# A six-layer windowed-attention stage in a new order of nine turns, with the queries' rotary halves added by an accumulating transfer

## What is computed

```python
def attn_layer(x, Wqkv, qs, ksc, Wo):            # 16 heads of 64, x first goes through shift_tokens
    q, k, v = jnp.split(x @ Wqkv, 3, -1)         # 128 -> 3 * 1024
    q = l2norm(q) * qs
    k = l2norm(k) * ksc
    q = q * cos * scale + rotate_half(q) * sin * scale
    k = k * cos * inv + rotate_half(k) * sin * inv
    out = local_attention(q, k, v)               # softmax over causal keys in a window of 32
    return out @ Wo

def ffn_layer(x, g, bln, W1, b1, W2, b2):        # x again through shift_tokens
    xn = (x - mu) / jnp.sqrt(var + 1e-05) * g + bln
    a, gate = jnp.split(xn @ W1 + b1, 2, -1)
    return a * jax.nn.gelu(gate, approximate=False) @ W2 + b2
```

## Time and profile before

| what | us |
|---|---|
| median of 2 runs | 3666.64 |
| lowest and highest | 3664.30, 3668.97 |
| the profiled execution, its own time | 3660.63 |
| span of the profiled execution | 3658.8 |
| granted TensorE clock, mean over the span | 0.991 of full speed |

### The profile page before, as it was taken

How to read it: one execution, slowest core, us unless ns; L and a number is a source line. 1 busy time by engine, 2 the same in 40 slices (tenths; PEclk the granted TensorE clock), 3 DMA queues, 4 the chain that set the end, 5 groups by cost and what they waited for, 6 DMA issues and landing times.

```text
span 3658.8 us, 125829 instructions
## 1 busy us (share of the span) xinstructions
PE 3573.9 (98%) x51141; PEld 2639.5 (72%) x51141; DVE 2813.3 (77%) x5297; ACT 2925.6 (80%) x5539; POOL 2587.4 (71%) x4812
## 2 busy tenths in 40 slices
PE   8989997999999999999999999999999999999997
PEld 6777884777777777777777777777777777777776
DVE  6834446888888888888888888888888888888884
ACT  5756664888888888888888888888888888888886
POOL 5522225777777777777777777777777777777773
PEclk9999999999999999999999999999999999999998
DMA  3000000000000000000000010000000000000000
GB/s 98 3 11 8 8 5 18 18 10 11 11 16 25 18 11 11 10 25 25 11 10 10 17 26 18 10 10 11 25 25 10 10 11 16 14 13 13 17 13 14
DMA packets 145113, 59.13 MB, mean 16 GB/s; under 512 B 117017, under 2 KB 139294, under 8 KB 144542
## 3 DMA queue, kind: packets, MB, share of 16 engines
q1 hardware_dynamic: 143820, 50.88, 5.6%
q10 hardware_dynamic: 722, 0.21, 0.0%
HBM read 23.95 MB, written 2.10 MB: 7 GB/s over the span
## 4 chain that ended last, share of the span: by engine, by line
PE 82%; DVE 1%; POOL 1%; ACT 0%; issue 0%; DMA 0%; SPq 0%; POOLq 0%; DVEq 0%
PE bank L1048 18%; PE bank L1021 11%; PE bank L1195 10%; PE bank L1100 10%; PE bank L1163 7%; PE bank L1179 6%; PE bank L1131 5%; PE bank L1116 5%; PE bank L1133 4%; PE bank L1039 3%; PE bank L1111 2%; DVE R L1353 0%; DVE ss L1368 0%; DMA ys<-Y 0%; POOL R L1466 0%
## 5 line engine op out<-in xcount | busy, mean ns | idle before, releaser
L1353 DVE TENSOR_TENSOR R<-bank,tables 128x1024 f32<-128x1024 f32 x768 | 903.5, 1218 | 218.6 <-ACT sq L1255 218.4
L1048 PE MATMUL bank<-WA,xcT 128*128 128x512 f32 x1536 | 693.9, 594 | 4.3 <-ACT xcT L1229 2.4
L1255 ACT ACTIVATE sq<-bank 128x512 f32<-128x512 f32 x768 | 459.2, 598 | 159.1 <-PE bank L1048 159.1
L1048 PEld LDWEIGHTS bank<-WA,xcT 128*128 128x128 f32 x1536 | 277.2, 190 | 283.2 <-issue 279.4
L1458 POOL TENSOR_TENSOR R<-R 128x512 f32<-128x512 f32 x384 | 480.4, 1272 | 0.0
L1368 DVE TENSOR_REDUCE ss<-sq 128x16 f32<-128x1024 f32 x384 | 459.8, 1198 | 0.2 <-issue 0.2
L1100 PE MATMUL bank<-WV,xcT 128*64 128x512 f32 x1536 | 414.2, 618 | 0.0
L1478 POOL TENSOR_TENSOR P<-P,inv_sum 128x512 f32<-128x512 f32 x384 | 401.6, 1046 | 0.7 <-DVE inv_sum L1408 0.7
L1472 POOL TENSOR_TENSOR P<-P,rn 128x512 f32<-128x512 f32 x384 | 402.0, 1047 | 0.0
L1195 PE MATMUL bank<-WO,OT 128*128 128x128 f32 x3072 | 396.8, 283 | 0.0
L1466 POOL TENSOR_TENSOR R<-R,rn 128x512 f32<-128x512 f32 x384 | 391.8, 1041 | 0.0
(11 more groups left out here) (157 smaller groups left out, 7819.6 us busy)
## 6 DMA issues: line engine op xcount, KB each, us to landing
WA<-in_wqkv SPq DMA_DIRECT2D x24, 256.0 KB, 2.9
ystat<-Y SPq DMA_DIRECT2D x192, 32.0 KB
ystat<-Y SPq DMA_DIRECT2D x384, 15.8 KB
ys<-Y SPq DMA_DIRECT2D x192, 32.0 KB
ys<-Y SPq DMA_DIRECT2D x384, 15.8 KB
WV<-in_wqkv SPq DMA_DIRECT2D x6, 512.0 KB, 3.8
WO<-in_wo SPq DMA_DIRECT2D x6, 512.0 KB, 4.5
X<-in_x SPq DMA_DIRECT2D x4, 512.0 KB, 5.2
```

Source lines behind the costliest of these rows:

```text
L1048: mm(b[QK_BANK[n, half]][:, :], m.xsT[:, k % 2, :], cols[:, half, :, :], start=True, stop=True)\
L1255: nc.scalar.activation(by_half[:, half, :, :], b[QK_BANK[n, half]][:, :].rearrange("p (h d) -> p h d", d=32), ACT.Square)\
L1353: tt(both, src.unsqueeze(1).to_broadcast([128, 2, 16, 32]), tab.unsqueeze(2).to_broadcast([128, 2, 16, 32]), ALU.mult).then_inc(s.rotated, 1)
```

## The change

The third stage is written anew; the first two stages are the same.

- **Queries' parts.** PE's accumulating second transposes are gone. Instead POOL issues one transfer in each turn, `queries_added`, which adds `R[:, QUERIES, 1, :]` onto `R[:, QUERIES, 0, :]` (128 partitions of 1024 fp32, 512 KB) with `accum_op`; `queries_turned`(i-1) waits for it one turn later and has eight passes instead of sixteen. `R` for the queries has one buffer, so the next tile's `rotary` waits for `queries_turned` half 0.
- **Keys' parts** are still added by two POOL instructions, but POOL scales the keys in the same turn i rather than at the head of turn i+1.
- **Order.** Every engine's list is new, PSUM's banks are assigned anew, and the pipeline is one turn deeper (LAST = 8, and the lists run for N + 9 turns).
- **Waits.** Semaphores with two or four parts in a turn are counted by a small class, and the increments `hold` are gone.

```diff
-FIRST, LAST = 0, 7
...
+LAST = 8
...
-    QK_BANK = {(QUERIES, 0): 1, (KEYS, 1): 0, (QUERIES, 1): 4, (KEYS, 0): 3}
-    TURNED_IN, TURNED_OUT = b[3], b[6]
-    KT_BANK, QT_BANK, V_BANK = (b[2], b[1]), (b[4], b[7]), (b[6], b[5])
-    S_BANK, PT_BANK, PV_BANK = (b[2], b[1]), (b[5], b[7]), (b[5], b[2])
-    OUT, FF_BANK, FF_OUT = b[1], (b[0], b[3], b[4]), b[0]
+    QK_BANK = {(QUERIES, 0): 3, (QUERIES, 1): 6, (KEYS, 0): 1, (KEYS, 1): 2}
+    TURNED_IN, TURNED_OUT = b[4], b[6]
+    KT_BANK, QT_BANK, V_BANK = (b[7], b[0]), (b[7], b[4]), (b[1], b[4])
+    S_BANK, PT_BANK, PV_BANK = (b[5], b[6]), (b[0], b[0]), (b[4], b[3])
+    OUT, FF_BANK, FF_OUT = b[0], (b[2], b[1], b[7]), b[5]
...
+            def queries_turned(t, j):
+                if exists(t):
+                    pe.wait_ge(s.q_added, 16 * t + 16)
+                    if j == 0:
+                        at_least(pe, s.h, 3 * (t - 6))
+                    elif t == N - 1:
+                        pe.wait_ge(s.v_copied.sem, s.v_copied.upto(1, t + 1))
                     for n in range(4):
...
+                        at = j * 512 + n * 128
+                        last = turned(QT_BANK[j][:, n * 128:(n + 1) * 128], m.R[:, QUERIES, 0, at:at + 128])
+                    last.then_inc(s.q_turned.sem, 1)
...
-                    for n in range(4):
-                        at, col = j * 512 + n * 128, n * 128
-                        mm(QT_BANK[j][:, col:col + 128], m.R[:, QUERIES, 0, at:at + 128], m.ident[:, :], is_transpose=True,
-                           start=True, stop=False)
-                        last = mm(QT_BANK[j][:, col:col + 128], m.R[:, QUERIES, 1, at:at + 128], m.ident[:, :],
-                                  is_transpose=True, start=False, stop=True)
-                    last.then_inc(s.q_turned, 1)
...
+            for i in range(N + LAST + 1):
+                input_turned(i)
+                out_projection(i - 5)
+                queries(i, 0)
+                queries_turned(i - 1, 1)
+                queries(i, 1)
+                queries_turned(i - 1, 0)
+                keys(i, 0)
+                keys(i, 1)
+                keys_turned(i - 1, 1)
+                keys_turned(i - 1, 0)
+                ff_out(i - 8)
+                probs_turned(i - 3, 1)
+                normal_turned(i - 6)
+                head_outputs(i - 4)
+                scores(i - 1)
+                values(i, 0)
+                values(i, 1)
+                probs_turned(i - 3, 0)
+                ff_in(i - 7)
...
+            for i in range(N + LAST + 1):
+                input_out(i)
+                gates(i - 8)
+                squares(i, QUERIES, 0)
+                squares(i, QUERIES, 1)
+                queries_out(i - 1, 0)
...
+                        if n == QUERIES:
+                            at_least(dve, s.q_turned.sem, s.q_turned.upto(0, t))
...
+            for i in range(N + LAST + 1):
+                rotary(i, QUERIES, 0)
+                rotary(i, QUERIES, 1)
+                statistics(i - 5)
+                squares_summed(i, QUERIES)
+                ff_added(i - 8)
+                rotary(i, KEYS, 0)
+                rotary(i, KEYS, 1)
+                squares_summed(i, KEYS)
+                seeded(i)
...
+            def queries_added(t):
+                if exists(t):
+                    pool.wait_ge(s.rotated.sem, s.rotated.upto((QUERIES, 1), t + 1))
+                    pool.dma_start(m.R[:, QUERIES, 0, :], m.R[:, QUERIES, 1, :], accum_op=ALU.add).then_inc(s.q_added, 16)
...
-            def turn(i, k):
-                keys_scaled(i - 1, k - 1, 0)
-                keys_scaled(i - 1, k - 1, 1)
-                scores_scaled(i - 2, k - 2, 0)
-                probs_scaled(i - 3, k - 3, 0)
-                scores_scaled(i - 2, k - 2, 1)
-                probs_scaled(i - 3, k - 3, 1)
-                inverse_deviation(i - 5, k - 5)
-                inverse_lengths(i, k)
                 keys_added(i, 0)
                 keys_added(i, 1)
...
+            for i in range(N + LAST + 1):
+                queries_added(i)
+                probs_scaled(i - 3, 0)
+                inverse_lengths(i)
+                keys_added(i, 0)
+                keys_added(i, 1)
+                keys_scaled(i, 0)
+                keys_scaled(i, 1)
+                scores_scaled(i - 1, 1)
+                probs_scaled(i - 2, 1)
+                scores_scaled(i - 1, 0)
+                inverse_deviation(i - 4)
```

More of the change, by code:

```diff
@@ L882, with __init__, upto @@
 STORED = 4
-FIRST, LAST = 0, 7
-def turns(eng, turn, n):
-    for i in range(n + LAST):
-        turn(i, i % 4)
-def inside(t, n):
-    return not isinstance(t, int) or 0 <= t < n
-def filling(t, n):
-    return isinstance(t, int) and t < n
-def draining(t, n):
-    return isinstance(t, int) and t >= n
+LAST = 8
+class Counted:
+    def __init__(self, sem, order):
+        self.sem, self.order = sem, order
+    def upto(self, part, tiles):
+        return len(self.order) * (tiles - 1) + self.order.index(part) + 1 if tiles > 0 else 0
 def local(nc, sem, m):
@@ L928, in local @@
[L928 to L932 removed]
+    s.qk, s.squared, s.rotated = counted("qk", *four), counted("squared", *four), counted("rotated", *four)
@@ L1379, in seeded @@
                     dve.wait_ge(s.seed, 3 * t + 2)
[L1380 removed]
+                    nc.vector.tensor_scalar(m.seed[:, t % 2, :], bits, -1.0, RSQRT_MAGIC, ALU.mult, ALU.add)\
                         .then_inc(s.seed, 1)
```

647 lines of the change are left out of this document (287 added, 360 removed).

## The result

The changed kernel takes 3621.23 us (median of 2 runs, 3621.16 to 3621.30) against 3666.64: a ratio of 0.9877 with a 95% interval of 0.9853 to 0.9901. It is 45 us faster, which is clear of no change but under 2%; the forecast was 3626. Measured again beside the experiments, 7 to 13 runs each time, the kernel before took 3661.86 to 3664.12, so 2.5 to 4.8 of the 45 us lie in its first two runs.

What follows compares the result with a forecast made beforehand. PE bounds the old kernel at 15.81 us a turn, Loop A the new one at 15.53: 3660.6 - 54 + 13 = 3620, with 6.0 for the median 3626 us. Range of 8 in 10: 3550 to 3790.

Steps and rivals of the forecast that it cites:

- I take 0.05 for each boundary: PE's new list has four more blocks, each boundary costing 0.05 us, 0.2 in all; PE alone would turn in 15.07 us.
- Loop A: Two-turn loop: two POOL scalings 2.00, PE 12.04, DVE 8.45, POOL 8.57; sum 31.06, so 15.53 us a turn, the slowest.
- Loop B: One-turn loop: keys scaled, keys' transposes, `ff_out`, DVE's addition, products and seed, then POOL 8.57: 15.03 us.
- Loop C: POOL itself: 13.92 us occupied plus the hold of the transfer's issue, 15.1 us a turn.
- g: Time the transfer's issue holds POOL, taken at 1.2 us between bounds of 0.71 and 2.46.
- Loop D: Two-turn loop through DVE, POOL, the transfer and PE's transposes back to `rotary`: 11.68 + (g + L)/2 us a turn.
- g + L: Time from POOL's start on the transfer's issue to its landing: taken at 7.0 us, bounds 3.8 and 10.0.
- rival 2: The transfer lands late, PE stands at `queries_turned` half 1, kernel slower: 3847 us at a landing of 10.0; chance 0.19.
- Hidden with 0.4 to spare: ACT's `gates` ahead of the squares: 4.8 us until DVE can start, against 5.2 by PE's second query transposes.
- The deeper pipeline: One turn more at the end of the stage; the last turns are 12.85 us apart, so 13 us more.
- PE stays the bound: Rival: PE alone sets the turn, at best 3538 us, over 2% faster from a turn of 15.36 down; chance 0.25.
- the long issue: Rival: the transfer's issue holds POOL too long, no gain at 1.8 us, 3789 us at 2.46; chance 0.11.

## Why the prediction was right, and where only by luck

**What goes.** Eight passes of the queries, forecast at 0.94, are 0.87 by the turns without a gap of the new order with sixteen and with eight. The boundaries, taken at 0.2, are not there: a half of the queries' transposes takes 0.43 (2013.98 to the next block at 2014.41), and the two blocks of values together 1.87 in place of 1.01 + 1.01. PE's own turn is 14.66 and not 15.07. Here the step "I take 0.05 for each boundary" failed, with its sign; it did not matter, since PE alone is not the bound.

**Loop A.** The mechanism is shown in its main part: PE waits for POOL's `P` at `probs_turned` half 1 (82 times), shortening POOL's serial stretch gives 91 us in this order and none in the old one, and opening both ways into DVE gives 40. Not as forecast is the way from PE to DVE. "DVE's `rotary` waiting for PE line 1008" holds for 20 turns in 2000 us; for 109 it is ACT:

```profile
DVE R L1319 <- ACT sq L1219: 85.0, 109, 1.1
DVE R L1319 <- PE bank L1008: 15.5, 20, 0.8
```

The size is right by errors that cancel, and that is luck. Every term was a little too high: PE 11.78 without its gap for 12.04, DVE 8.19 for 8.45, POOL 8.24 for 8.57 (its twelve small operations 3.73 for 4.07), 15.18 together for 15.53. Against that stand two things that I had not foreseen, PE's gap in one turn of three and DVE's wait at `ssm`. They cannot simply be added to loop A, which passes `scores` once in two turns: with a gap of 1.0 in one pass of three it would stand at (30.37 + 0.33) / 2 = 15.35. The chain takes the way that meets every gap, loop A and a turn of PE alone: (30.37 + 14.66 + 1.0 + 0.46) / 3 = 15.50, and 15.54 was measured. The forecast had taken the longest loop by itself; its own warning, that loops close to each other may add up, came near to this. The circuit of three turns is read from the chain. That it has this length since the gap comes once in three turns fits, but no run varied how often the gap comes with the rest in place.

**Loop B** was forecast at 15.03 and never ended last in the changed kernel: DVE stands idle for 0.2 us in all before its addition (line 1300) in 2000 us. It stands close behind, for at 2034.43 the addition starts 0.21 after `ff_out` has ended, and it comes out once A is cut (117 waits). So that cutting A gives only 40 us is due in part to B; the price of each way was not separated.

**Loop C and the issue.** g was taken at 1.2; the issue and what it adds to the next scaling are 0.97 (POOL's end of `nmr` at 2020.20 to the end of the scaling at 2022.17, less 1.00 for a plain one). C is then 14.9 and no bound. But "C is no bound" is not "the issue is free": every turn it stands ahead of `probs_scaled` on POOL, this scaling then runs while DVE wants its `ssm`, and the issue is worth most of 24 us.

**Loop D and the landing.** g + L was taken at 7.0; it is 4.7, so D is 11.68 + 2.35 = 14.0, and rival 2 is far off: with a landing of 2.3 nothing changes. The bound of 10.0 was a load queued behind others; the median rows at 3.8 and 4.5 were the nearer guide. The reading that an accumulating transfer moves twice as much was right for the engines' share: 14.7% against 7.0%, 2.1 times. The Trainium skill (Collectives: The Full Stack, section The bandwidth ceiling) says of the add in a ReduceScatter that it needs two source reads and so halves the rate; in the engines' share this trace agrees. In time to landing it is 4.7 against 3.6. The fit of the Trainium skill (DMA: Bandwidth & Descriptors, section Anatomy of one DMA — SWDGE (gpsimd) path) gives an estimate of 3.2; the plain copy is 0.4 above it. The forecast feared that DVE would hold up POOL's issue, by a port that they share. That isn't seen: g came out under its value, and the issue takes 0.94 to 0.96 in every turn from 1000 to 2000 us. What is seen is the other direction, DVE's `ssm` behind POOL's scaling.

**ACT.** "Hidden with 0.4 to spare": in the turn above DVE's `rotary` started at 2015.98, released by ACT's square, while PE's transposes had ended at 2015.88. The margin is gone by 0.1, and without the table loads the time is the same. PE was quicker than I had it, ACT was not.

**The deeper pipeline.** Forecast +13 us. From the first `ystat` transpose to the last:

```profile
L1021 PE MATMUL bank<-ident,ystat x192: 272/273/476, 570.1 to 3577.2; 128*128 128x128 f32 x192
```

```profile
L1008 PE MATMUL bank<-ident,ystat x192: 299/299/475, 571.1 to 3536.2; 128*128 128x128 f32 x192
```

3007.1 before and 2965.1 after: 42 us less for 191 turns, not 54. What follows the last is 3658.8 - 3577.2 = 81.6 before and 3619.5 - 3536.2 = 83.3 after. So the end costs 2 us more and not 13; why so little was not looked into. Last, 6 us were added because the median of before stood 6.0 above its profiled execution; after, it is 3621.23 against 3621.30. The forecast took 54 off and added 13 and 6, 35 in all; measured from one profiled execution to the other it is 39. These errors cancel also.

**The rivals.** "PE stays the bound" is excluded, with PE at 94% and waits in two turns of three, as are the late transfer and the long issue. Of the signs, PE busy near 96% came out at 94%, and "almost no idle time" on POOL was wrong for the turn shown: it stood 2.00 us before the seed, as a loop over more than one turn allows. What the four rivals lacked was a stop inside PE's own stream.

**Where the 180 us went.** The passes are worth 0.94 a turn to PE. In the new order 0.18 of 0.87 comes through, the rest goes to loop A with the gap and `ssm`; in the old order 0.31 does (15.82 - 15.51), and DVE's one-turn loop takes the rest. The new order did not make the whole loss. Had I worked out the old order's loop through DVE with eight passes, I should have seen that it stood at 15.5 too. Of kernels with the full computation the best here is the one with `values` between the small matmuls, 3594.56.

**What PE's gap is.** The page of each kernel has a DMA queue of the kind "instruction" (packets, MB, share). Here it is before, then after:

```profile
q8 instruction: 412, 6.75, 0.8%
...
q8 instruction: 400, 6.55, 0.8%
```

These are packets of 16 KB, and 12 fewer of them go with 1536 matmuls and 1536 weight loads fewer, so a packet stands for 3072 / 12 = 256 instructions of PE. From 1000 to 3000 us there are 217 of them after the change, 1.69 a turn, which is five in three turns. By their times in the trace they come some 9 us apart, and every one of the 44 gaps in `scores` ends 1.2 to 1.6 us after one of them has landed. The same holds in each of the eight other kernels that have such gaps. And the stop goes by the count of instructions: where it comes in every third turn it comes some 6 matmuls earlier each time (9, 15, 22, 28, 35 and 41 matmuls are left behind it, from 1323 us on), at the same places with two Newton steps, where the times differ. With sixteen passes PE has eight more in a turn and 1.75 packets, seven in four turns, and there the stop comes in every fourth turn, 2 matmuls later each time (7, 5, 3, 1 left, in the turns from 1382 us on). So PE stops because its next instructions have not arrived. That is read from the traces; no run changed the supply itself.

**What stays open.** Why the supply falls behind only around the two blocks of small matmuls, and how long a row of them it bears: with two Newton steps the gaps are 37.5 us in 2000 side by side and 26.2 with four transposes between; with 512-column products between there are none. Why DVE's `ssm` has to wait for POOL. And how the 56 us that the run with the second buffer fell short divide between loop B, `ssm` and the gap.

## What to carry to other kernels

Before you price an instruction that is removed, walk each loop of waits in the old order with it gone: here 0.94 us off the bound was worth 0.3 in the old order and 0.2 in the new, since a loop through DVE stood just behind in the one and loops through POOL in the other. Look for the serial stretch on the loop, even of tiny operations: four POOL operations of 0.2 us gave more (91 us) than eight PE passes (34 us). A loop need not be the one that you wrote down: follow the recorded chain until it is back at its start, and count the turns. And a total that agrees is no proof of its terms: read each term again in the new trace.

## What the runs showed that I had not expected

- PE stops for about 1.0 us (at most 1.6) in one turn of three where two blocks of 64 matmuls of 64 columns stand side by side, 43.8 us in 2000; with 512-column products between them the same matmuls show none. Each stop ends 1.2 to 1.6 us after a 16 KB packet of instructions has landed.
- An accumulating transfer of 512 KB within the on-chip buffer shows 0.94 us at POOL's issue, a plain copy 0.64. POOL's next operation, 1.0 us of work, ends 2.03 after the start of the one and 1.73 after the start of the other.
- The accumulating transfer lands in 4.7 us, the plain copy in 3.6, and one of 8 KB still takes 2.3.
- A DVE operation of 128 x 32, 0.18 us by itself, that starts while POOL's operation behind the accumulating issue runs ends only about 0.05 after it: 0.48 us on average.
